# Two-layer GNN on one core: layer 1's first gathers and copy issued from layer 0's program, its last eight batches merged over four tiles, a ring of 17 batches

## The reference

```python
deg = jnp.maximum(segment_sum(jnp.ones(dst.shape), dst, num_segments=100000), 1.0)
deg_isqrt = deg ** (-0.5)
h = jnp.maximum(_layernorm(x, axis=-1), 0.0)            # x: (100000, 256) float32
x = x + deg_isqrt[:, None] * segment_sum((deg_isqrt[:, None] * h)[dst] * edge_weight[:, None], src, ...)
h = jnp.maximum(_layernorm(x, axis=-1), 0.0)
feat = jnp.concatenate([h[dst], h[src] - h[dst]], axis=-1)        # 25,000 edges
msg = jax.nn.relu(feat @ W1 + b1) @ W2 + b2                       # 512 -> 512 -> 256
x = x + segment_sum(msg, dst, ...) / (segment_sum(ones, dst, ...) + 1e-8)
```

## Time and profile before

| | us |
|---|---|
| median of 3 runs | 2072.03 (2069.7 to 2079.29) |
| profiled execution, its own time | 2073.74 |
| its span | 2071.6 |
| PE busy | 1675.2 (81%) |
| DVE busy | 1467.4 (71%) |
| POOL busy | 1275.0 (62%) |
| ACT busy | 1009.0 (49%) |
| layer 0's scatters, first to last start | 413.3 to 939.8 |
| layer 1's first instruction | 949.3 |
| layer 1's scatters, first to last start | 1341.8 to 2061.3 |

### The profile page before, as it was taken

One profiled execution on the slowest core, in us unless ns is written; L12 is line 12 of the kernel. 1 busy time (PEld: TensorE's weight loads), 2 busy tenths in 40 slices (PEclk: granted clock), 3 DMA queues, 4 the chain that ended last, 5 costly groups with the idle time before them and its releaser, 6 DMA issues.

```text
span 2071.6 us, 46204 instructions
## 1 busy us (share of the span) xinstructions
PE 1675.2 (81%) x13740; PEld 1472.9 (71%) x13740; DVE 1467.4 (71%) x5883; ACT 1009.0 (49%) x2064; POOL 1275.0 (62%) x1004
## 2 busy tenths in 40 slices
PE   4957878888888556520899999999999999999991
PEld 1237768888887556420788888898888888888881
DVE  6967879999998466510777777777667677676660
ACT  0004445545554223211576766666657566566560
POOL 2036661078888877864443444488888888888854
PEclk9978999999999777755999999999999999999996
DMA  7989999866666555547999999745555455555543
GB/s 240 317 298 362 352 354 341 269 109 113 111 110 110 94 98 97 90 54 237 339 334 340 337 338 341 247 91 98 91 91 99 91 98 94 93 97 93 94 65 38
DMA packets 140467, 376.43 MB, mean 182 GB/s; under 512 B 31391, under 2 KB 95656, under 8 KB 127528
## 3 DMA queue, kind: packets, MB, share of 16 engines
q0 software_dynamic: 84672, 128.51, 35.0%
q1 hardware_dynamic: 27452, 208.63, 27.6%
q10 hardware_dynamic: 28304, 38.85, 7.0%
HBM read 323.36 MB, written 258.12 MB: 281 GB/s over the span
## 4 chain that ended last, share of the span: by engine, by line
PE 22%; POOL 18%; issue 8%; DMA 4%; DVE 1%; ACT 0%; ACTq 0%; POOLq 0%; DVEq 0%
PE ps_h L1268 13%; POOL table_out L956 10%; POOL ends L944 9%; PE ps_m L1282 6%; DMA table_out<-e_ring,e_targets_all 3%; PE ps_s L1295 2%; PE ps_t L1255 2%; DMA ends<-x,keys 1%; DVE e_moments L1018 0%; ACT e_ring L1199 0%; DVE out_sum L1090 0%; ACT hid L1181 0%; ACT feat_hi L1174 0%; DVE out_lo L1095 0%; ACTq L1152 0%
## 5 line engine op out<-in xcount | busy, mean ns | idle before, releaser
L944 POOL DMA_INDIRECT ends<-x,keys x392 | 402.2, 1026 | 305.0 <-PE ps_h L1268 107.6
L468 POOL DMA_INDIRECT x<-slots,targets_all x196 | 327.0, 1668 | 179.7 <-DVE targets_all L631 96.9
L956 POOL DMA_INDIRECT table_out<-e_ring,e_targets_all x196 | 322.5, 1645 | 91.9 <-issue 54.1
L793 PE MATMUL ps_deg<-table,hot 128*128 128x128 bf16 x5488 | 318.2, 220 | 29.1 <-DVE hot L536 29.1
L793 PEld LDWEIGHTS ps_deg<-table,hot 128*128 128x128 bf16 x5488 | 309.8, 98 | 33.4 <-issue 19.9
L1268 PE MATMUL ps_h<-feat_hi,w_hi 128*128 128x512 f32 x784 | 314.6, 401 | 10.9 <-DVE feat_lo L1085 5.7
L1268 PE MATMUL ps_h<-feat_hi,w_lo 128*128 128x512 f32 x784 | 310.5, 396 | 0.0
L807 PE MATMUL ps_sum<-msg_hi,same 128*128 128x260 f32 x784 | 159.4, 336 | 186.8 <-issue 179.3
L1268 PE MATMUL ps_h<-feat_lo,w_hi 128*128 128x512 f32 x784 | 310.4, 396 | 0.0
L807 PEld LDWEIGHTS ps_sum<-msg_hi,same 128*128 128x128 f32 x784 | 135.7, 238 | 193.9 <-issue 193.9
L453 POOL DMA_INDIRECT slots<-in_x,row_idx x196 | 209.4, 1068 | 96.2 <-issue 55.8
(11 more groups left out here) (141 smaller groups left out, 3458.0 us busy)
## 6 DMA issues: line engine op xcount, KB each, us to landing
table_out<-x SPq DMA_DIRECT2D x400, 252.0 KB
x<-in_x SPq DMA_DIRECT2D x400, 250.0 KB
hi_row<-hi_rows ACTq DMA_DIRECT2D x49, 256.0 KB
src_row<-src_rows ACTq DMA_DIRECT2D x49, 256.0 KB
dst_row<-dst_rows ACTq DMA_DIRECT2D x49, 256.0 KB, 3.5
ends<-x,keys POOLq DMA_INDIRECT x392
slots<-in_x,row_idx POOLq DMA_INDIRECT x196
x<-slots,targets_all POOLq DMA_INDIRECT x196
```

Source lines behind the costliest of these rows:

```text
L468: pool.indirect_dma_start(out=x1_d, out_offset=bass.IndirectOffsetOnAxis(ap=targets_all[:, b, j:j + 1], axis=0), in_=slots[:, b % SLOTS, j ...
L793: last = nc.tensor.matmul(ps_deg[q][k][:, j * P:(j + 1) * P], hot[:, c, k, j * P:(j + 1) * P], table[:, c, part, :], start=(c == 0 and par ...
L944: pool.indirect_dma_start(out=ends[b % NE][:, n, :], out_offset=None, in_=x1_d, in_offset=bass.IndirectOffsetOnAxis(ap=keys[:, 1 - end, at ...
L956: pool.indirect_dma_start(out=out, out_offset=bass.IndirectOffsetOnAxis(ap=e_targets_all[:, b, j:j + 1], axis=0), in_=e_ring[:, b % RING1, ...
```

## The change

- `ends[0]` gets a place of its own that lives through layer 0 too. POOL issues the 8 gathers of layer 1's batch 0 at the end of its layer 0 list, behind the last landing and ahead of the barrier. Layer 1's list begins with batch 1.
- SP issues the first 8 pieces of layer 1's copy at the end of its layer 0 list, behind a wait for all scatters; the other 392 stay in layer 1's list.
- DVE's `feat_low(0, k)` moves ahead of batch 1's moments.
- Batches 41 to 48 (`TAIL`) merge over all 4 tiles: `peers` and `after` are 512 wide, `sums` has 32 matmuls instead of 16, its first group waits for both `out_lo`, and POOL waits for landings once a batch, not twice. The steps 41 to 44 are written out now, as 45 to 48 were.
- To make room: `SLOTS` 30 to 28, `LEAD0` 28 to 27, `RING1` 20 to 17.

```diff
-    SLOTS = 30
-    RING1 = 20
+    SLOTS = 28
+    RING1 = 17
+
+    TAIL = 41
     NE = 4
-    LEAD0 = 28
+    LEAD0 = 27
     AHEAD0 = 16
     LEAD1 = 20
...
+                sp.wait_ge(scattered, 16 * W * NB)
+                for k in range(FLIGHT):
+                    sp.dma_start(out_flat[k], x1_flat[k]).then_inc(bulk_out[k], 16)
+
...
+                for n in range(2 * W):
+                    pool.indirect_dma_start(
+                        out=ends0[:, n, :], out_offset=None, in_=x1_d,
+                        in_offset=bass.IndirectOffsetOnAxis(ap=keys[:, 1 - n // W, n % W:n % W + 1], axis=0))\
+                        .then_inc(ends0_in, 16)
...
-            QUADS = (NB - 1) // NE - 1
+            QUADS = (TAIL - 1) // NE
+
+            def merged(b):
+
+                return W if isinstance(b, int) and b >= TAIL else G
...
-                for k in range(FLIGHT):
-                    sp.dma_start(out_flat[k], x1_flat[k]).then_inc(bulk_out[k], 16)
                 with sp.Fori(1, ROUNDS) as r:
...
-                    pool.wait_ge(e_scattered, 16 * G * (GROUPS * b + g + 1))
+                    if (g + 1) * G % merged(b) == 0:
+                        pool.wait_ge(e_scattered, 16 * G * (GROUPS * b + g + 1))
...
-                for b in range(LEAD1):
+                for b in range(1, LEAD1):
...
+                    M = merged(b)
                     for j in range(W):
-                        g = j // G
-                        last = nc.vector.tensor_scalar(peers[q][:, j, :], dst_row[q][:, g * G * P:(g + 1) * G * P],
+                        w = j // M
+                        last = nc.vector.tensor_scalar(peers[q][:, j, 0:M * P], dst_row[q][:, w * M * P:(w + 1) * M * P],
                                                        dst_col[q][:, j:j + 1], None, ALU.is_equal)
...
                     if b == 0:
                         scales_of(*whole(0))
-                for k in range(KF):
-                    feat_low(0, k)
+                        for k in range(KF):
+                            feat_low(0, k)
...
+                    M = merged(b)
                     for g in range(GROUPS):
-                        pe.wait_ge(out_lo_done, GROUPS * b + g + 1)
+                        pe.wait_ge(out_lo_done, GROUPS * b + (g + 1 if M == G else GROUPS))
 
                         pe.wait_ge(e_in_ring, GROUPS * b + g + 1)
-                        for a in range(G):
+                        for a in range(G * g, G * g + G):
+                            w = a // M * M
```

More of the change, by code:

```diff
@@ L856, in gnn_preln_two_layers @@
             inv_deg = [sb(f"inv_deg{q}", [P, W], fp32) for q in range(2)]
-            peers = [sb(f"peers{q}", [P, W, G * P], fp32r) for q in range(2)]
-            after = sb("after", [P, G, G * P], bf16)
-            peers_after = sb("peers_after", [P, W, G * P], bf16)
+            peers = [sb(f"peers{q}", [P, W, W * P], fp32r) for q in range(2)]
+            after = sb("after", [P, W, W * P], bf16)
+            peers_after = sb("peers_after", [P, W, W * P], bf16)
             n_after = sb("n_after", [P, W], fp32)
@@ L1007, in _ @@
                 dve.wait_ge(after_made, 1)
[L1008 to L1010 removed]
+                for a in range(W):
+                    if a + 1 < W:
+                        nc.vector.memset(after[:, a, (a + 1) * P:W * P], 1.0)
+                    last = nc.vector.tensor_copy(after[:, a, a * P:(a + 1) * P], later[:])
+                last.then_inc(after_made, 1)
                 dve.wait_ge(after_made, 2)
```

26 lines of the change are left out of this document (13 added, 13 removed).

## The result

The changed kernel takes **2049.38 us** (median of 4 runs, 2045.44 to 2051.28), the kernel before 2072.51 on the same chip (4 runs, 2069.7 to 2079.29): ratio 0.9882, 95% interval 0.9857 to 0.9907. The prediction was 2048, range 2041 to 2057.

The account below looks back on a forecast made before the run. It took PE's pace to bound layer 1 until 1341.8, then POOL, which alone sets the end. -8.3 (first scatter) - 15.7 (tail) = -24.0 gives 2049.7 in the profiled frame, 2048 as a median; range 2041 to 2057.

Parts of the forecast that it names:

- Layer 0's shorter lead: Layer 0: two more steps hold gathers (+2.0), the copy loses 1.6 us of company; +1 taken, bounds 0 and +3.
- Layer 1's start: Border of the layers: eight gathers ahead of POOL's drain start layer 1 at 959.2 instead of 949.33, later by 9.9.
- Landing of batch 0's rows: Border: rows land 9.4 us behind the last gather, at about 962.1; batch 0's moments start some 6.3 earlier.
- `feat_low` and batch 1: Start of layer 1: batch 1's moments gain only 6, first `mlp_out` some 12 us earlier, carried on by PE's pace.
- The copy replaces PE: Layer 1's first scatter: it waits for the copy, not PE's pace, and starts at 1333.5, 8.3 earlier; bounds 2 and 11.
- The 3 us for late semaphores: End of layer 1's copy: its last pieces' semaphores reach POOL 0 to 4 us later; 3 taken.
- The ring of 17: Layer 1's first scatters: slot 17 is wanted in step 18, so no stall, with about 14 us to spare.
- The tail: End of layer 1: four scatters with one wait take 10.3 a batch, not 12.8; 15.7 saved, bounds 13 and 19.
- What PE pays: Last batches: longer `sums` and last merge delay batch 48's results by 3.3 plus 0 to 6.4; just hidden.
- The middle: First scatter of layer 1 to last gather: shifts as one piece of 639 us, with no gain or loss counted.
- POOL is held up by wider DVE instructions: Rival, chance 0.04: scatters of batches 42 to 46 take longer beside DVE, up to +10 us, 2058.
- The rival of the drain: Border, chance 0.14: drain waits until the gathers have landed; layer 1 starts at 967.4, time 2055.

Follow-up runs that it names:

- e4: The kernel before with only the smaller sizes (SLOTS 28, LEAD0 27, RING1 17): 2072.71 us, ratio 0.9992 to before.
- e1: The changed kernel with every batch merged over two tiles again, border and sizes kept: 2060.56 us, ratio 0.9938 to before.
- e11: The changed kernel with batches 33 to 48, not 41 to 48, merged over four tiles: 2050.94 us, ratio 0.9902 to before.
- e8: The changed kernel with 16 early copy pieces, not 8, and DVE's set-up of `after` behind batch 0's scales: 2096.85 us on the slower chip, ratio 0.9898 to before.
- e9: The changed kernel with the first eight copy pieces back in layer 1's list, early gathers kept: 2109.17 us (1 run, slower chip).
- e2: The kernel before with only the last eight batches merged over four tiles and the ring of 17: 2058.31 us, ratio 0.9935 to before.
- e7: The changed kernel with 16 instead of 8 copy pieces ahead of the barrier: 2107.02 us on the slower chip, ratio 0.9934 to before.
- e12: The changed kernel with eight more copy pieces in layer 0's program, issued once the early gathers have landed: 2050.05 us, ratio 0.9887 to before.
- e13: The changed kernel with eight more pieces behind the early gathers' landing and DVE's set-up behind batch 0's scales: 2048.04 us, ratio 0.9882 to before.
- e6: The changed kernel with batch 0's eight gathers back behind the barrier, early copy pieces kept: 2102.37 us (1 run, slower chip).

## Why the prediction was right, step by step

**Layer 0's shorter lead: not resolved.** +1 was predicted, and the averages above give 0.8, but single profiles lie 8 us apart. The 1.6 that the profile after shows as a gain is in the next profile of the same kernel too, while e4, with the same sizes, ends 0.9 later than before. That the total fits does not test this term.

**Layer 1's start: right.** 959.2 predicted, on the layer 0 of before; 957.96 measured, with a layer 0 that ended 1.6 earlier: 19.4 against 19.8 behind its last scatter.

**Landing of batch 0's rows: wrong, and the moments met by luck.** 962.1 was predicted from the 9.4 of the earlier trace rows; the last rows moved at 954.1, 3.0 behind the last gather's start. In the kernel before, SP kept feeding pieces beside the gathers; now nothing follows the eight. DVE's set-up, which the prediction had end at the same time, took the place of the rows: it ended at 960.6, and no wait for rows stands ahead of the moments. So they start 22.5 behind layer 0's last scatter, where 22.3 was said.

**`feat_low` and batch 1: right in mechanism, a little small.** Batch 1's moments gained 9.2, not 6 (984.10 to 974.92, 17 behind layer 1's start instead of 19), and `mlp_out` 16.3, of which 14.6 is not layer 0's, where 12 was said. Against layer 0's end, the pace at the first scatter gained 12.5 and 11.1 in two profiles, where 12.3 was said: some 2 to 3 us of what `mlp_out` had gained were lost on the way, against "PE's own pace then carries this", and the two errors nearly cancel.

**The copy replaces PE: right.** The first scatter waits for the copy in all four profiles with this border (2.63, 1.53, 4.28 in e1, 6.02 in e11). 1333.5 was predicted, which is 9.3 ahead of before with layer 0 taken out; 10.2, 9.8, 8.0 and 7.2 were measured. The 3 us for late semaphores had no row behind it and was too much: wherever the copy is waited for, the scatter starts 1.3 to 1.4 behind the copy's last packet (these four, e8 and e9). The copy itself ended later than forecast, 390.4 to 393.5 behind layer 0's last scatter instead of 389.9, so that the two errors partly cancel. It ended 389.3 behind in the kernel before: SP's early start of 7.0 us bought nothing against that kernel, where "about 1 us" was said. Against a kernel with the early gathers but without the early pieces it is worth over 10: e9 has its first scatter at 404.8, though on another chip.

**The ring of 17: right**, no stall in any profile.

**The tail: right.** 15.7 predicted, 14.8 measured (14.7 in e2, against before). The prediction's own terms add up to 15.6, a slip of 0.1. The rest is the batch: 10.46, not 10.3, five times, since several scatters took 1.7 to 2.0 instead of 1.55. What PE pays came out near the top of its bounds: batch 48's results 695.4 behind the first scatter, before 686.7, so 8.7 later where 3.3 + 0 to 6.4 was said. 4.4 us are left of the cover.

**The middle: an effect that the sum had at nothing.** It "shifts as one piece of 639 us", and longer scatters in it were named as a sign of being wrong; that sign showed. Where nothing merges over four tiles the middle is 636.2 to 639.7, in the kernels on the same chips that merge 640.1 to 642.1. Two effects overlap in this. From the first scatter to the 41st, 153.4 to 153.9 us pass on these chips where PE sets the first one, and 151.1 to 152.1 where the copy does (on the slower chip 150.5 to 151.7 either way). From the 121st scatter to the 161st, 149.6 to 149.8 us pass in the profiles without merging, and 151.6 to 152.0 in all ten with it; from there to the last gather another 1 us or so is lost (33.7 before, 35.0 and 34.7 in the two profiles of the changed kernel). So with the start alike, merging costs some 3 us in the middle (e2 against before: 642.0 against 638.9), and the quicker start makes it look like 1.5. In e11, whose wide instructions begin eight batches earlier, the 40 scatters ahead of the 121st take 151.5 too, where all others show 150.3 to 150.6. POOL's idle time is the same (122 us in sum in both). Its instructions take longer. Groups of lines from 1860 to 1965, before:

```profile
L956 POOL DMA_INDIRECT table_out<-e_ring,e_targets_all x29 | 47.2, 1626 | 8.8 <-issue 8.5 <-DMA table_out<-e_ring,e_targets_all 0.3
L944 POOL DMA_INDIRECT ends<-x,keys x39 | 39.3, 1007 | 11.9 <-issue 11.6 <-DMA table_out<-e_ring,e_targets_all 0.3
L1047 DVE TENSOR_SCALAR peers<-dst_row,dst_col 128x256 fp32r<-128x256 f32 x20 | 6.3, 378 | 0.1
```

And after:

```profile
L975 POOL DMA_INDIRECT table_out<-e_ring,e_targets_all x28 | 46.2, 1650 | 8.5 <-issue 8.5
L963 POOL DMA_INDIRECT ends<-x,keys x38 | 39.7, 1046 | 11.6 <-issue 11.3 <-DMA table_out<-e_ring,e_targets_all 0.3
L1079 DVE SCALAR_TENSOR_TENSOR peers_after<-dst_row,dst_col,after 128x512 bf16<-128x512 f32 x19 | 13.1, 747 | 0.0
L1070 DVE TENSOR_SCALAR peers<-dst_row,dst_col 128x512 fp32r<-128x512 f32 x20 | 8.8, 502 | 0.0
```

38 x 0.039 + 28 x 0.024 = 2.2 us. This is the rival "POOL is held up by wider DVE instructions", which was given 0.04: it is there in every merging kernel, at 2 us in these 40 scatters and the gathers between them, not at 10. The traces say where the time goes. Paired one by one with those of before, POOL's 95 scatters and gathers from the 121st scatter on take 2.04 us longer. 1.47 of this falls on the 27 that run beside a `peers` or `peers_after` instruction, 54 ns each. Of the 0.57 on the other 68, 0.50 is one gather, the longest (1519 ns at 1854.68), which stands beside `hid_lo` and no widened instruction; it is as long in the second profile (1496), and its cause stays open. In e1, which merges over four tiles nowhere, the same sum is 0.10. In the tail the 20 scatters of batches 43 to 47 take 0.6 longer than in the kernel before, but the longest of them (1966 ns) stands beside none of these instructions, and before had one of 2007; that part is not put down to the rival. The Trainium skill, "SBUF — State Buffer", section "Who interferes with whom", says that DVE's tensor_scalar can enter a two-port mode, and that DVE in such a mode and GpSimd shut each other out for a whole instruction. That POOL is delayed beside these instructions fits; that it waits for whole ones is not what the mean shows (54 ns, where one `peers` takes 502). No run here took `peers` alone away, so how much is due to which of the two DVE instructions stays open.

**The rival of the drain (0.14) was half right.** In the changed kernel it cost nothing: the gathers' last data moved at 954.1, and the drain's 5.3 us behind the last gather ended at 957.3. But e7 and e8 show that a drain does wait for POOL's gathers, so the forecast of layer 1's start came true by an early landing that the prediction did not foresee. With its own 962.1 for the landing, and the 3 us that the drain took behind the data in e7 and e8, layer 1 would by an estimate have started at about 965 instead of 959.2. The Trainium skill, "Perfetto Trace Analysis", section "DMA Instruction — SWDGE (GPSIMD)", lets such an instruction end when its descriptors are written; this trace agrees for the gather's own row (0.95 us, its data later), and by e7 the drain is not covered by that.

**The chances** for a faster kernel add up to 0.94 as they stand, not 0.91; nothing hangs on it.

## What to carry to other kernels

Work moved ahead of a barrier moves the barrier: count what every engine still issues ahead of it, SP's plain copies too (0.6 us a piece, e12), and ask whether transfers are left in flight that the drain waits for (e7). Two streams that meet at one wait have to move together: the early gathers without the early copy gain nothing (e9), and a copy that ends earlier gains nothing where the barrier holds back the other stream (e13). A wait for landings is worth merging only where nothing covers it, so at the end of the list; further up, the same merge only adds work (e11).

## What the hardware showed unexpectedly

- POOL's drain at a block's end took 4.63 to 5.28 us with POOL's own transfers landed (e4, e6; before). With eight gathers ahead of it, it ended 5.3 us behind the last of them in seven profiles, where by the DMA packets their data moved until 1.5 to 2.0 behind it, and 10.5 behind in e7 and 10.4 in e8, where the data moved until 7.4 and 7.2 behind it. SP's transfers did not hold it (e6, e12).
- PE's last merge of the changed kernel ran at half the full clock at first. It had idled 2.22 us for the second `out_lo`; then four matmuls took 1.03 us, and 0.64 five groups later. Stretches of it, granted clock third from the end:

```profile
2016.00:2019.00 3.00, 3.00 (x28) 3.00 (x27) 1.38 (x2) 1.36 (x3) 1.25 (x1) 1.00 0.75 84
2022.00:2025.00 3.00, 3.00 (x16) 3.00 (x15) 0.00 (x0) 0.00 (x0) 2.46 (x2) 0.50 0.62 61
```

  From 2.4 to 1.2 GHz for some 3.5 us: (1.03 - 0.64) x 4 = 1.6 us of the 8.7 above. All ten profiles that merge have the same 2.22 us of idle time ahead of this merge; the granted clock fell to 0.50 in five of them (both of the changed kernel, e7, e11, e12) and stayed at 1.00 in the other five. In e2, one of these, four matmuls took 0.64 from the second group on, and its results were as late (695.9). So the idle time does not always bring the clock down, and the clock did not decide anything here.
- On the slower chip PE stood still for 3.3 to 3.5 us in batch 0's `mlp_in` with no releaser shown (e6, e9), and in all four profiles there `mlp_out` came 16.0 to 19.4 behind batch 1's moments instead of 13.5 to 14.0. The cause stays open; it is the reason why e6 and e9 are read by their waits and against each other.
